# Last delta round computes five chunks of the output projection, heads in three slots by GpSimd's queue, semaphores cleared inside the phases

## The chip, the cores and the metric

The kernel runs on one core of a Trainium2 chip. The metric is the device time of one execution in microseconds. The engines are named PE (TensorE), DVE (VectorE), ACT (ScalarE), POOL (GpSimd) and SP (SyncE, which only issues DMAs here). Each runs its own queue of instructions in order, and waits on semaphores for the others.

## The reference

All in float32, on x of shape 4 x 512 x 512. Each of the four steps adds a layer-normalised result to x:

```python
x = x + ln(ssm(ln(x)))          # diagonal state space layer
x = x + ln(moe(ln(x)))          # 8 experts, top 2, and a shared one
x = x + ln(delta(ln(x)))        # below
x = x + ln(ffn(ln(x)))          # below
# delta: 16 heads of 128, 4 batches of 512 tokens
#   q,k,v = silu(conv(x @ W));  S = a*S - b*(S k - v) k^T;  o = S q
#   o = (layernorm(o) * ln_w + ln_b) * sigmoid(x @ Wg);  return o @ Wo      # Wo: 2048 x 512
# ffn: logits = x[batch].reshape(-1) @ switch_w.T + switch_b   (8 experts, over a whole batch of 512 tokens)
#   top 2 experts of the batch; per head of 32 columns: gelu(xh @ w1.T + b1) @ w2.T + b2, weighted, summed
#   return (x + o) @ w3.T + b3
```

## The kernel before

The tokens lie in 16 chunks of 128 tokens (NT = 16, TPB = 4 chunks a batch). The program is a sequence of phases: SSM, shared expert, routed experts, MoE output, delta, output. Each is a block in which every engine has a program of its own, and ends with a barrier of all engines. Names begin with a_, b_, x_, o_, c_ and d_ in that order. Between phases `retire_sems` opens one more block, in which GpSimd clears the semaphores of the phase that ended (L79), and all engines meet again (L75). That is done at four places.

The delta phase (`phase_delta`) works in 16 rounds, each of HG = 4 heads over one batch of 4 chunks, and stores the gated and transposed heads (c_oT) to the DRAM tensor ot_d. In its last round PE has no further projections to do; in their slots it computes the output projection (`out_part`) of chunks 0 to AHEAD - 1. One chunk is 16 heads x one matmul 128x512, four per weight tile (c_xs, c_w_k, c_w_q, c_w_v), here called a group. Its inputs are loaded into the tiles c_kT, c_qT, c_vT, its result sits in a PSUM bank c_ps_pj and is kept by ACT in c_conv. The end of the last round is, for each of the four chunks of batch 3: DVE's statistics, ACT's `norm_apply` (L1887), POOL's `gate_out` (L1563, three operations: times ln_w, plus ln_b, times the gate), PE's `turn_out` (transposes, L1670), ACT's `store` (L1876, L1879).

The output phase (`phase_out`) takes the chunks in order. PE: `outputs(n)` (the remaining projections, L2324, into yo[n % 2]), `turn(n)` (transposes of the normalised x, L2334), `route_logits(b)` after a batch, `chosen_experts(b)`, and the last layer. DVE per chunk: statistics of y (d_y_st), the residual add into d_x (L2521), statistics of x, and eight products with the switch weights (d_product, L2509), which make the routing logits; per batch the choice of experts (`choose`, d_w_sel, d_w_diag). ACT: the roots and the two activations per chunk (d_yn, d_xn), the copies of transposes and the gelus. `outputs(n)` waits until chunk n - 2 is normalised (y_normed), since that frees its bank. The experts of batch 0 stand inside chunk EARLY = 14. SP loads heads for chunk n + 2 once chunk n - 1 or so is projected (L2247), in one queue with the stores of x (L2258), and loads the switch weights, 2 MB for each of four parts.

Of the kernel before, what the change touches and what calls it, by code (L numbers as in the profile page):

```python
# [51 lines left out]
AHEAD = 3  # L52


class Program:


    def __init__(self, nc, io):
        self.nc, self.io = nc, io
        self.lasting = ExitStack()  # L60
        self.waits_passed = self.lasting.enter_context(nc.semaphore("waits_passed"))
        self.phase_sems = []
# [10 lines left out]
    def retire_sems(self):  # L73

        with self.nc.Block() as block:  # L75
            @block.gpsimd
            def _(e):
                for s in self.phase_sems:
                    e.sem_clear(s)  # L79
        for s in self.phase_sems:  # L80
            self.nc.release_semaphore(s)
        self.phase_sems = []
# [541 lines left out]
def phase_moe_shared(pr, con, XT, w_gu, gu_loaded, rt):  # L624
# [3 lines left out]
    with ExitStack() as st:  # L628
# [66 lines left out]
        def _(e):  # L695
# [23 lines left out]
            e.dma_start(rt.token[:, :], io["slot_token"].rearrange("(p t) o -> p (t o)", p=P)).then_inc(token_loaded, 16)  # L719

# [284 lines left out]
class DeltaInput:  # L1005
# [13 lines left out]

    def heads_out(self, n):  # L1020
        tile = self.heads["kqv"[n]] if n < AHEAD else self.heads["kq"[n % 2]]
        return tile[:, :, :].rearrange("p h (c m) -> p (h c) m", m=P)


def phase_moe_out(pr, con, XT, rt, tab, first):
# [6 lines left out]
    with ExitStack() as st:  # L1032
# [62 lines left out]
        def _(e):  # L1095
            for b in range(NB):
                if b >= 2:
                    e.wait_ge(y_done, TPB * (b - 1))
                for c in range(TPB):
                    for k in range(2):  # L1100
                        n = b * TPB + c
                        e.indirect_dma_start(picked[b % 2][k][:, c, :], None, io["y_slots"].rearrange("t p d -> (t p) d"),
                                             bass.IndirectOffsetOnAxis(rt.slot[:, k, n:n + 1], 0)).then_inc(picked_loaded[b % 2][c], 16)

# [222 lines left out]
def phase_delta(pr, con, XT, tab, given):  # L1327
# [15 lines left out]
    with ExitStack() as st:  # L1343
# [88 lines left out]
        ahead_bank = [pj[0], pj[1], pj[0]]  # L1432
# [13 lines left out]
        def _(e):  # L1446
# [63 lines left out]
            e.wait_ge(ahead_ready, 2)  # L1510
            load_ahead(3)
            e.wait_ge(ot_stored, rounds_before(NR - NB + 2))
            load_ahead(4)
            for n in (3, 4):
# [3 lines left out]
        def _(e):  # L1518
# [61 lines left out]
            def tail(r, buf):  # L1580
                a_round(r, buf, last=True)
                for c in range(TPB):
                    gate_out(r, buf, c)
# [23 lines left out]
            rounds(e, lambda r, buf, half: a_round(r, buf), tail)  # L1607

        @block.tensor
        def _(e):  # L1610
# [39 lines left out]
            def out_part(n, of):  # L1650
                for h in of:
                    if h == 0:
                        e.wait_ge(ahead_loaded[n], 16)
                        if n == 0:
                            e.wait_ge(conv_step, TAP_STEPS * (CONVS * (NR - 1) + CONVS + 1))
                        else:
                            e.wait_ge(g_copied, TPB * (NR - 1) + HG - 2 + n)
# [15 lines left out]
            def a_round(r, buf, half, last=False):  # L1673
# [3 lines left out]
                def next_unit(u, halves_=(0, 1)):  # L1677
# [4 lines left out]
                    for half_ in halves_:  # L1682
                        h = v * HG + half_ * HG // 2
                        if h < AHEAD * NH:
                            out_part(h // NH, range(h % NH, h % NH + HG // 2))
# [160 lines left out]
            def tail(r, buf):  # L1846
                a_round(r, buf, None, last=True)
                for c in range(TPB):
                    turn_out(r, c)

# [3 lines left out]
        def _(e):  # L1854
# [35 lines left out]
            def keep(n):  # L1890
                e.wait_ge(ahead_ready, n + 1)
                e.activation(conv[:, n, :], ahead_bank[n][:, :], ACT.Copy).then_inc(ahead_kept, 1)
# [851 lines left out]
```

## Time and profile before

| what | value |
|---|---|
| median of 3 runs | 3209.87 us (3209.33 to 3214.2) |
| the profiled execution's own time | 3214.72 us |
| span in its trace | 3213.0 us |
| mean granted TensorE clock | 0.950 |
| barriers that end the SSM, routed experts, MoE output and delta phases | 455.7, 1093.4, 1223.5, 2870.5 us |
| output phase | 2876.6 us to 3213.0 us |

Start times are counted from the first instruction of the span. A new phase begins a few microseconds after each of the four barriers.

### The profile page before, as it was taken

The numbers are of one execution on the slowest core, as the hardware profiler recorded it, in microseconds if no ns is written. First come the engines' busy times: TensorE is split into PE (matmuls) and PEld (weight loads), VectorE is DVE, ScalarE is ACT, GpSimd is POOL, SyncE is SP. The second block draws the span as 40 slices with busy tenths as digits, with TensorE's granted clock in tenths as the row PEclk, the third lists the DMA queues.
The fourth block names the chain that finished last, engine by engine and source line by source line (L and its number), as shares of the span: only waits on it lengthen the run. The fifth ranks groups of instructions, "written<-read, shape, count | busy, mean of one in ns | idle before, by whom it ended". The sixth has DMA issues, their size and how long they took to land. (4 is left out here: it accounts for less than half of the span.)

```text
span 3213.0 us, 42340 instructions
## 1 busy us (share of the span) xinstructions
PE 2944.2 (92%) x13274; PEld 1661.0 (52%) x13275; DVE 1882.8 (59%) x4723; ACT 1204.9 (38%) x2189; POOL 625.9 (19%) x759
## 2 busy tenths in 40 slices
PE   7899979997999588999999999999999999968998
PEld 3344444444666344666556665566555665533443
DVE  5767741000111276777787777867788777626766
ACT  3545500001222145444554445534554354422232
POOL 1111203101111312122222223222231222320000
PEclk9999968998999889999999999999999999979999
DMA  3000142003222451001100011000110001225312
GB/s 118 26 14 27 40 176 96 20 13 124 65 65 65 159 215 68 1 28 54 44 24 15 28 53 44 24 15 28 50 45 27 15 28 50 80 79 195 106 36 92
DMA packets 77123, 197.09 MB, mean 61 GB/s; under 512 B 11376, under 2 KB 12032, under 8 KB 70272
## 3 DMA queue, kind: packets, MB, share of 16 engines
q1 hardware_dynamic: 59744, 158.84, 13.8%
q0 software_dynamic: 6816, 18.92, 1.8%
q10 hardware_dynamic: 10368, 16.83, 1.4%
q8 instruction: 111, 1.82, 0.2%
q14 instruction: 84, 0.69, 0.1%
HBM read 137.90 MB, written 56.66 MB: 61 GB/s over the span
## 5 line engine op out<-in xcount | busy, mean ns | idle before, releaser
L2027 DVE SCALAR_TENSOR_TENSOR c_conv<-c_ps_pj,c_conv_t,c_conv 128x511 f32<-128x511 f32 (+2 forms) x495 | 367.9, 746 | 86.3 <-ACT c_conv L1866 74.7
L1647 PE MATMUL c_ps_pj<-c_w_g,c_xs 128*128 128x512 f32 x512 | 227.6, 592 | 0.0
L1630 PE MATMUL c_ps_pj<-c_xs,c_w_v 128*128 128x512 f32 x480 | 225.8, 593 | 0.0
L1630 PE MATMUL c_ps_pj<-c_xs,c_w_k 128*128 128x512 f32 x480 | 216.0, 593 | 2.9 <-DMA c_xs<-xt_d 2.9
L1630 PE MATMUL c_ps_pj<-c_xs,c_w_q 128*128 128x512 f32 x360 | 192.4, 668 | 2.2 <-DVE c_conv L2027 2.0
L1866 ACT ACTIVATE c_conv<-c_ps_pj,c_conv_t 128x512 f32<-128x512 f32 x165 | 127.8, 775 | 90.5 <-PE c_ps_pj L1630 83.9
L997 DVE TENSOR_TENSOR x_act<-x_hs,x_ps_u 128x352 f32<-128x352 f32 x40 | 20.9, 521 | 226.9 <-ACT x_hs L982 226.9
L1647 PEld LDWEIGHTS c_ps_pj<-c_w_g,c_xs 128*128 128x128 f32 x512 | 94.8, 190 | 107.1 <-issue 107.1
L2042 DVE TENSOR_TENSOR c_block_t<-c_block_L,c_block_X 128x126 f32<-128x126 f32 (+22 forms) x496 | 137.4, 277 | 18.5 <-DVE c_block_X L2046 1.8
L2046 DVE TENSOR_TENSOR c_block_X<-c_block_X,c_block_t 128x126 f32<-128x126 f32 (+22 forms) x496 | 137.6, 277 | 17.0
L850 DVE TENSOR_TENSOR b_act<-b_hs,b_ps_u 128x512 f32<-128x512 f32 (+1 forms) x24 | 16.5, 686 | 205.9 <-PE b_ps_u L742 205.9
L1630 PEld LDWEIGHTS c_ps_pj<-c_xs,c_w_k 128*128 128x128 f32 x480 | 86.5, 190 | 89.2 <-issue 86.1
L1920 ACT ACTIVATE c_err<-c_negL 32x128 f32<-32x128 f32 x256 | 78.6, 307 | 135.2 <-DVE c_negL L2115 130.5
L1696 PE MATMUL c_ps_kk<-c_kT 128*128 128x128 f32 x512 | 102.8, 283 | 26.3 <-DVE XT L2117 16.1
L261 PE MATMUL a_ps_pj<-XT,a_w_in 128*128 128x512 f32 x256 | 121.3, 619 | 3.5 <-DVE a_conv L486 2.7
L241 POOL TENSOR_SCALAR a_skip<-a_xc,a_col_d 128x512 f32<-128x512 f32 x32 | 62.6, 1956 | 316.3 <-ACT a_xc L355 174.3
L948 PE MATMUL x_ps_g<-b_w_gu,x_xT 128*128 x320 | 122.4, 464 | 1.4 <-ACT x_xT L973 0.8
L949 PE MATMUL x_ps_u<-b_w_gu,x_xT 128*128 x320 | 122.0, 463 | 0.0
L1563 POOL TENSOR_TENSOR XT<-XT,c_ln_w 128x512 f32<-128x512 f32 x64 | 81.2, 1269 | 195.3 <-DVE c_block_L L2048 157.5
L267 PE MATMUL a_ps_gt<-XT,a_w_gate 128*128 128x512 f32 x256 | 115.3, 593 | 2.5 <-ACT a_th L347 2.5
L1696 PEld LDWEIGHTS c_ps_kk<-c_kT 128*128 128x128 f32 x512 | 82.4, 195 | 64.1 <-DVE XT L2117 35.4
L284 PE MATMUL a_ps_yo<-a_w_out,a_th 128*128 128x512 f32 x256 | 115.5, 603 | 0.0
(433 smaller groups left out, 6094.3 us busy)
## 6 DMA issues: line engine op xcount, KB each, us to landing
c_xs<-xt_d SPq DMA_DIRECT2D x16, 1024.0 KB, 4.9
ot_d<-c_oT ACTq DMA_DIRECT2D x64, 256.0 KB, 2.0
b_w_gu<-in_w_gu SPq DMA_DIRECT2D x8, 1408.0 KB, 23.6
y_slots<-x_y SPq DMA_DIRECT2D x40, 256.0 KB, 2.0
a_x<-in_x SPq DMA_DIRECT2D x8, 1024.0 KB, 6.5
c_qT<-ot_d SPq DMA_DIRECT2D x8, 1024.0 KB, 5.6
d_x<-x SPq DMA_DIRECT2D x32, 256.0 KB, 2.9
d_switch<-in_switch_w SPq DMA_DIRECT2D x4, 2048.0 KB, 14.7
```

What stands on the lines that cost most here:

```text
L261: mm = e.matmul(pj[c % 2][:, :], w_in[:, k, c * P:(c + 1) * P], XT[:, b, k, :], start=(k == 0), stop=(k == KD - 1))
L267: mm = e.matmul(gt[:, :], w_gate[:, k, c * P:(c + 1) * P], XT[:, b, k, :], start=(k == 0), stop=(k == KD - 1))
L284: mm = e.matmul(yo[t % 2][:, :], th[:, b % 2, c, t * P:(t + 1) * P], w_out[:, c, :], start=(c == 0), stop=(c == CT - 1))
L948: e.matmul(g_ps[par][:, 0:FE], xT[par][:, k, :], w_gu[:, expert, k, 0:FE], start=(k == 0), stop=(k == KD - 1))
L949: mm = e.matmul(u_ps[par][:, 0:FE], xT[par][:, k, :], w_gu[:, expert, k, FE:2 * FE], start=(k == 0), stop=(k == KD - 1))
L1630: mm = e.matmul(bank_of[xb][u][:, :], w["kqv"[u // HG]][:, k, (u % HG) * DH:(u % HG + 1) * DH], xs[xb][:, k, :], start=(k == 0), stop=(k = ...
L1647: mm = e.matmul(pj[(xb + i) % 2][:, :], xs[xb][:, k, i * P:(i + 1) * P], w["g"][:, k, :], start=(k == 0), stop=(k == KD - 1))
L1696: e.matmul(kk[:, h, :], chunk(kT, h, c), chunk(kT, h, c), start=True, stop=True)
L1866: e.activation(conv[:, u % 4, :], bank_of[buf][u][:, :], ACT.Identity, bias=conv_t[buf][:, m, h, TAPS:TAPS + 1], scale=conv_t[buf][:, m, h ...
L2027: e.scalar_tensor_tensor(oc, bank_of[buf][u][:, 0:SEQ - s], conv_t[buf][:, m, h, TAPS - 1 - s:TAPS - s], oc, ALU.mult, ALU.add).then_inc(c ...
L2042: e.tensor_tensor(t, block_L[:, i + 1:BB, i].unsqueeze(2).to_broadcast([P, n, k]), block_X[:, i, 0:k].unsqueeze(1).to_broadcast([P, n, k]) ...
L2046: e.tensor_tensor(below, below, t, ALU.add).then_inc(sub_step, 1)
```

## The change

- Clearing: `retire_sems` has no block of its own; the semaphores of a phase are cleared by GpSimd at the end of its program in the phase after (`clear_retired`), in the shared expert's, the MoE output's and the delta phase. The delta phase's own are not cleared.
- AHEAD is 5. The last delta round computes chunks 0 to 4; part of chunk 3 and all of chunk 4 stand between and behind the transposes of the last round. Chunk 4 is kept in c_w_g.
- The last round's gating is DVE's.
- Heads for chunks 7 to 15 are loaded by GpSimd's queue into three tiles.
- In the output phase chunks 5 to 10 have a PSUM bank each (six banks), later ones alternate; transposes have fixed places among the groups; the experts of batch 0 stand before chunk 13 and wait until chunk 10 is normalised; ACT's and DVE's part of them stands before chunk 11; ACT does the y activation of chunk n before it copies the transposes of n - 1.
- w3 is loaded after the store of chunk 5.

```diff
-AHEAD = 3
+AHEAD = 5
     def retire_sems(self):
-        with self.nc.Block() as block:
-            @block.gpsimd
-            def _(e):
-                for s in self.phase_sems:
-                    e.sem_clear(s)
-        for s in self.phase_sems:
+        for s in self.cleared_sems:
             self.nc.release_semaphore(s)
-        self.phase_sems = []
+        self.cleared_sems, self.retired_sems, self.phase_sems = [], self.phase_sems, []
+    def clear_retired(self, e):
+        for s in self.retired_sems:
+            e.sem_clear(s)
+        self.cleared_sems, self.retired_sems = self.retired_sems, []
...
+    @staticmethod
+    def slot_out(n):
+        return "kqv"[n % 3] if n < 11 else "kq"[(n + 1) % 2]
+    def kept_out(self, n):
+        return self.conv[:, n, :] if n < 4 else self.w["g"][:, n - 4, :]
...
-        ahead_bank = [pj[0], pj[1], pj[0]]
+        ahead_bank = [pj[n % 2] for n in range(AHEAD)]
...
             def tail(r, buf):
                 a_round(r, buf, None, last=True)
-                for c in range(TPB):
+                out_part(3, range(HG, NH))
+                for c in range(2):
                     turn_out(r, c)
+                out_part(4, range(NH // 2))
+                for c in range(2, TPB):
+                    turn_out(r, c)
+                out_part(4, range(NH // 2, NH))
...
                 for c in range(TPB):
                     norm_apply(r, c)
+                keep(3)
                 for c in range(TPB):
                     store(r * TPB + c, ot_round[r, c])
+                keep(4)
...
-    EARLY = NT - 2
+    EARLY = AHEAD + 6
...
+        ring = [yo[0], yo[1], h_ps[0], h_ps[1], o_ps[0], o_ps[1]]
+        bank = {n: ring[n - AHEAD] if n < AHEAD + 6 else yo[(n - AHEAD) % 2] for n in range(AHEAD, NT)}
...
+            for n in range(AHEAD + 2, NT):
+                last_user = max(m for m in range(n) if given.slot_out(m) == given.slot_out(n))
+                if last_user >= AHEAD:
+                    e.wait_ge(yo_ready, last_user + 1)
+                e.dma_start(given.heads_out(n).rearrange("p (g h) m -> p g h m", h=HG),
+                            io["ot_d"].rearrange("g b c p h m -> b c p g h m")[n // TPB, n % TPB]).then_inc(heads_loaded[given.slot_out(n)], 16)
...
                 if of[0] == 0:
-                    e.wait_ge(heads_loaded[n % 2], 16 * (n // 2 + 1))
                     if n >= AHEAD + 2:
+                        e.wait_ge(heads_loaded[given.slot_out(n)], 16 * loads_of(n))
+                    if n >= AHEAD + 8:
                         e.wait_ge(y_normed, n - 1)
+                    elif n >= AHEAD + 6:
+                        e.wait_ge(y_normed, n - 5)
...
+                if b == 0:
+                    e.wait_ge(y_normed, AHEAD + 6)
...
+            turned_before = {HG + 3 * v: v for v in range(NT - 4)}
+            turned_before.update({10 * HG: NT - 4, 10 * HG + 2: NT - 3})
+            logits_after = {(9, 1): 0, (12, NG - 1): 1, (14, NG - 1): 2}
...
+                scale_y(n)
                 if n > 0:
                     take_turned(n - 1)
-                scale_y(n)
```

On PE, at the end of the delta phase, before the change (c_ps_kk is the last matmul of the round, c_ps_d the transposes of `turn_out`, L1343 the end of the phase):

```order
1004 L1823 MATMUL c_ps_z<-XT,c_R 128x128 x4
1005 L1840 MATMUL c_ps_kk<-c_err,XT 128x128 x4
1006 L1670 MATMUL c_ps_d<-ident,XT 128x128 x16
1007 L1343 UNCONDITIONAL_BRANCH
1008 L2316 UNCONDITIONAL_BRANCH
```

and with the change (c_ps_pj is the output projection, of chunk 3 from c_kT and of chunk 4 from c_qT):

```order
1004 L1832 MATMUL c_ps_z<-XT,c_R 128x128 x4
1005 L1670 MATMUL c_ps_pj<-c_xs,c_kT 128x512 x2
1006 L1849 MATMUL c_ps_kk<-c_err,XT 128x128 x4
1007 L1670 MATMUL c_ps_pj<-c_xs,c_kT 128x512 x2
1008 L1670 MATMUL c_ps_pj<-c_w_k,c_kT 128x512 x4
1009 L1670 MATMUL c_ps_pj<-c_w_q,c_kT 128x512 x4
1010 L1670 MATMUL c_ps_pj<-c_w_v,c_kT 128x512 x4
1011 L1680 MATMUL c_ps_d<-ident,XT 128x128 x8
1012 L1670 MATMUL c_ps_pj<-c_xs,c_qT 128x512 x4
1013 L1670 MATMUL c_ps_pj<-c_w_k,c_qT 128x512 x4
1014 L1680 MATMUL c_ps_d<-ident,XT 128x128 x8
1015 L1670 MATMUL c_ps_pj<-c_w_q,c_qT 128x512 x4
```

The transposes, one run of 16 before, now stand in two runs of 8 with 8 matmuls of chunk 4 between them and 8 behind (the last row and one more like it).

On PE, where the experts of batch 0 stand in the output phase, before (d_ps_h and d_ps_o are the experts' two layers, c_kT holds chunk 14's heads):

```order
1068 L2341 MATMUL d_ps_logits<-d_part,ones 128x32
1069 L2324 MATMUL d_ps_yo<-c_xs,c_kT 128x512 x4
1070 L2324 MATMUL d_ps_yo<-c_w_k,c_kT 128x512 x4
1071 L2324 MATMUL d_ps_yo<-c_w_q,c_kT 128x512 x4
1072 L2348 MATMUL d_ps_h<-XT,d_w_diag 128x512 x4
1073 L2359 MATMUL d_ps_o<-c_conv,d_w_diag 128x512 x2
```

and with the change (c_qT holds chunk 12's heads, c_kT chunk 13's):

```order
1060 L2361 MATMUL d_ps_tp<-ident,d_xn 128x128 x4
1061 L2351 MATMUL d_ps_yo<-c_w_v,c_qT 128x512 x4
1062 L2368 MATMUL d_ps_logits<-d_part,ones 128x32
1063 L2375 MATMUL d_ps_h<-XT,d_w_diag 128x512 x4
1064 L2386 MATMUL d_ps_o<-c_conv,d_w_diag 128x512 x2
```

The experts moved from chunk 14's last group to the place between chunks 12 and 13, right behind the second batch's logits.

On POOL, at the end of the delta phase and the start of the output phase, before:

```order
242 L1563 TENSOR_TENSOR XT<-XT,c_gate 128x512
243 L1343 UNCONDITIONAL_BRANCH
244 L76 UNCONDITIONAL_BRANCH
245 L79 ISA x78
246 L75 UNCONDITIONAL_BRANCH
247 L2307 UNCONDITIONAL_BRANCH
248 L2310 MEMSET d_r_prefer 128x1 x8
```

and with the change (the ISA rows are the clears):

```order
223 L1572 TENSOR_TENSOR XT<-XT,c_gate 128x512
224 L82 ISA x38
225 L1352 UNCONDITIONAL_BRANCH
226 L2325 UNCONDITIONAL_BRANCH
227 L2328 MEMSET d_r_prefer 128x1 x8
228 L2329 MEMSET d_same_head 128x128
229 L2332 MEMSET d_same_head 32x32 x4
230 L2337 DMA c_qT<-ot_d 128x4x512
231 L2337 DMA c_vT<-ot_d 128x4x512
232 L2337 DMA c_kT<-ot_d 128x4x512
```

The 78 clears are gone, 38 stand before the end of the phase, and nine loads of heads follow the memsets, of which three are shown.

## Rows read from the trace of the kernel before

**Rows 1.** The page: busy time, share of the span and instructions of each engine.

```profile
PE 2944.2 (92%) x13274; PEld 1661.0 (52%) x13275; DVE 1882.8 (59%) x4723; ACT 1204.9 (38%) x2189; POOL 625.9 (19%) x759
```

**Rows 2.** Barriers and clears by line: duration ns, then first and last start in us.

```profile
L137 PEldq EVENT_SEMAPHORE  x1: 51/51/51, 455.7 to 455.7; - x1
L858 PEldq EVENT_SEMAPHORE  x1: 51/51/51, 1093.4 to 1093.4; - x1
L1032 PEldq EVENT_SEMAPHORE  x1: 51/51/51, 1223.5 to 1223.5; - x1
L1343 PEldq EVENT_SEMAPHORE  x1: 51/51/51, 2870.5 to 2870.5; - x1
L79 POOLq EVENT_SEMAPHORE_RANGE_CLEAR  x188: 44/44/48, 455.8 to 2876.0; - x188
L75 PEldq EVENT_SEMAPHORE  x4: 51/51/51, 458.7 to 2876.6; - x4
```

**Rows 3.** The timeline behind two barriers: start us, us, engine, line, operation.

```profile
1096.10 0.40 SPq L1071 DMA_DIRECT2D o_shared<-y_shared  x1
...
1226.57 0.34 SPq L1447 DMA_DIRECT2D c_ln_w<-in_ln_w  x1
```

**Rows 4.** The timeline of the delta phase's end; in brackets the idle time before.

```profile
2840.38 1.16 PE L1840 MATMUL c_ps_kk<-c_err,XT 128*128 128x128 f32 x8 [0.69 <-ACT c_err L1979]
...
2847.88 6.26 ACT L1887 ACTIVATE XT<-XT,c_o_nb,c_o_rs 128x128 f32<-128x128 f32 x16 [7.06 <-DVE c_o_nb L2094]
...
2853.93 1.12 PE L1670 MATMUL c_ps_d<-ident,XT 128*128 128x128 f32 x4 [12.39 <-POOL XT L1563]
...
2864.94 1.26 POOL L1563 TENSOR_TENSOR XT<-XT,c_gate 128x512 f32<-128x512 f32 x1 [0.18 <-POOL XT L1563]
...
2866.26 1.11 PE L1670 MATMUL c_ps_d<-ident,XT 128*128 128x128 f32 x4 [2.99 <-POOL XT L1563]
2867.41 0.60 ACT L1876 ACTIVATE c_oT<-c_ps_d 128x512 f32<-128x512 f32 x1 [3.51 <-PE c_ps_d L1670]
```

**Rows 5.** The timeline of PE in the output phase's first 46 us.

```profile
2876.74 6.47 PE L2324 MATMUL d_ps_yo<-c_xs,c_qT 128*128 128x512 f32 x8 [9.37 <-SPq L2277]
...
2912.40 0.66 PE L2334 MATMUL d_ps_tp<-ident,d_xn 128*128 128x128 f32 x4 [4.27 <-ACT d_xn L2432]
2922.22 5.93 PE L2324 MATMUL d_ps_yo<-c_xs,c_qT 128*128 128x512 f32 x8 [9.16 <-DMA c_qT<-ot_d]
```

**Rows 6.** The timeline of ACT (first row) and DVE in the output phase.

```profile
2876.63 1.28 ACT L2463 ACT_TABLE_LOAD   x1 [8.62 <-PEq L75]
...
2890.70 0.69 DVE L2509 SCALAR_TENSOR_TENSOR d_product<-d_xn,d_switch 128x512 f32<-128x512 f32 x1 [6.64 <-DMA d_switch<-in_switch_w]
...
2976.76 0.42 DVE L2558 TENSOR_TENSOR d_chosen<-d_w,d_r_one 128x256 f32<-128x256 f32 x1
...
2982.61 0.69 DVE L2490 BATCH_NORM_STATS2 d_y_st<-d_ps_yo 128x6 f32<-128x512 f32 x1
...
2987.36 0.69 DVE L2521 TENSOR_TENSOR d_x<-d_x,d_yn 128x512 f32<-128x512 f32 x1 [0.98 <-ACT d_yn L2432]
...
2991.70 0.15 DVE L2496 SCALAR_TENSOR_TENSOR d_x_nb<-d_x_mv,d_x_rs 128x1 f32<-128x1 f32 x1
```

**Rows 7.** The chain that ended last, in order of time: start us, us, what.

```profile
2982.15 13.74 PE d_ps_yo L2324 x32
...
3077.68 3.43 PE d_ps_yo L2324 x8
...
3095.33 0.71 DVE d_y_st L2490
```

**Rows 8.** Windows: us, busy time of each engine, granted clock, DMA share, GB/s.

```profile
2854.00:2870.00 16.00, 4.39 (x16) 2.79 (x16) 0.00 (x0) 2.53 (x5) 11.13 (x9) 0.50 0.17 66
2884.00:2908.00 24.00, 24.00 (x63) 10.77 (x61) 12.09 (x35) 5.05 (x12) 0.00 (x0) 1.00 1.04 369
```

**Rows 9.** DMA issues: out<-in, engine, count, KB each, median us to landing.

```profile
c_qT<-ot_d SPq DMA_DIRECT2D x8, 1024.0 KB, 5.6
...
x_x<-xn,x_one_token POOLq DMA_INDIRECT x40, 3.4
...
c_w_g<-in_w SPq DMA_DIRECT2D x1, 1024.0 KB, 15.4
```

More of the change, by code:

```diff
@@ L1509, in _ @@
             load_ahead(2)
-            e.wait_ge(ahead_ready, 2)
-            load_ahead(3)
             e.wait_ge(ot_stored, rounds_before(NR - NB + 2))
-            load_ahead(4)
-            for n in (3, 4):
+            for n in range(3, AHEAD + 2):
+                e.wait_ge(ahead_ready, n - 2)
+                load_ahead(n)
+            for n in (AHEAD, AHEAD + 1):
                 e.wait_ge(ahead_loaded[n], 16)
@@ L1891, in keep @@
                 e.wait_ge(ahead_ready, n + 1)
-                e.activation(conv[:, n, :], ahead_bank[n][:, :], ACT.Copy).then_inc(ahead_kept, 1)
+                e.activation(given.kept_out(n), ahead_bank[n][:, :], ACT.Copy).then_inc(ahead_kept, 1)
             ot_round = io["ot_d"].rearrange("g b c p h m -> (g b) c p h m")
@@ L2175, in tail @@
                     norm_part(r, c)
+                e.wait_ge(ln_loaded, 32)
+                for c in range(TPB):
+                    n = r * TPB + c
+                    e.wait_ge(o_normed, HG * n + HG)
+                    e.wait_ge(g_done, n + 1)
+                    for i, (b, op) in enumerate(((over_heads(ln_w), ALU.mult), (over_heads(ln_b), ALU.add), (gates[buf][:, c], ALU.mult))):
+                        if i > 0:
+                            e.wait_ge(o_gated, 3 * n + i)
+                        e.tensor_tensor(o[:, c], o[:, c], b, op).then_inc(o_gated, 1)
             rounds(e, a_round, tail)
@@ L2221, in phase_out @@
         o_ps = [ps(f"o{i}", [P, SEQ]) for i in range(2)]
-        z_ps = [yo[0], yo[1], o_ps[0], o_ps[1]]
-        heads_loaded = [sem(f"heads_loaded{i}") for i in range(2)]
+        z_ps = [yo[1], yo[0], o_ps[0], o_ps[1]]
+        ring = [yo[0], yo[1], h_ps[0], h_ps[1], o_ps[0], o_ps[1]]
+        bank = {n: ring[n - AHEAD] if n < AHEAD + 6 else yo[(n - AHEAD) % 2] for n in range(AHEAD, NT)}
+        heads_loaded = {m: pr.swdge_sem(f"d_heads_{m}_loaded") for m in "kqv"}
+        loads_of = lambda n: sum(given.slot_out(m) == given.slot_out(n) for m in range(AHEAD + 2, n + 1))
         x_loaded = [sem(f"x_loaded{c}") for c in range(TPB)]
@@ L2239, in phase_out @@
         block = st.enter_context(nc.Block())
-        source = lambda n: kept[:, n, :] if n < AHEAD else yo[n % 2][:, :]
+        source = lambda n: given.kept_out(n) if n < AHEAD else bank[n][:, :]
         row = lambda name, n: io[name][n // TPB, n % TPB * P:(n % TPB + 1) * P, :]
```

66 lines of the change are left out of this document (24 added, 42 removed).

## The prediction

> **What bounds the kernel now.** I read the page first: TensorE (PE) is busy 92% of the span, VectorE (DVE) 59% [rows 1]. So only two things can shorten the kernel: stretches in which PE does nothing, and PE work at less than full clock. I then went to the four places the diff touches and read, at each, which wait ends last.
>
> The first kind is the end of a phase. By the rows of the barriers, all engines have met at 455.7, 1093.4, 1223.5 and 2870.5 us, then GpSimd clears 188 semaphores, and the next phase begins at 458.7, 1096.1, about 1226.5 and 2876.6 [rows 2, 3]. Nothing else runs there. The four gaps are 2.94, 2.68, 2.96 and 6.08 us, 14.66 in all; the second and third ends are those of the next phase's first DMA issue less some 0.06.
>
> The second is the end of the delta phase. PE's last real matmul group starts at 2840.38; DVE's statistics end at 2847.9, ScalarE (ACT) normalises, and POOL gates each chunk in three operations of 1.27 us, 4.1 us a chunk. Each transpose waits for that, the last store follows 2867.4, and the barrier is at 2870.5 [rows 4]. PE is busy 4.4 of 16 us, its clock at 0.50, the lower of its two levels [rows 8].
>
> The third is the output phase up to chunk 15's last matmul, when its statistics start (3095.33 [rows 7]): 218.7 us from 2876.6. A chunk costs PE 13.74 us, and the experts of the first batch half from 3063.76 to 3077.68, 13.9 us [rows 7]. PE's work is 13 x 13.74 + 15 turns x 0.44 + 13.9 + 0.6 for logits = 199.7. The rest: a wait of 4.27 us for ACT and one of 9.16 us for chunk 5's heads [rows 5], together 13.4, and groups of 8 matmuls at low clock, 6.47 and 5.93 us where 3.43 (13.74 / 4) is normal, 3.0 + 2.5 = 5.5. That adds up to 218.6. DVE meanwhile needs 9.27 us per chunk (2982.61 to 2991.85), 5.9 us to choose a batch's weights and some 3.8 for its routing [rows 6], so it stays under PE's 14.2 a chunk and waits for it.
>
> **The change, term by term.**
>
> *Clears.* 110 of the clears move behind GpSimd's last instruction of three phases; the delta phase's 78 vanish. GpSimd has long been idle at the end of the first two, and in the last its work shrinks, since the 12 gating operations leave it. Covered by PE's remaining work, they cost nothing; uncovered, 38 would cost about 3 us each time. I take -14.7.
>
> *Delta tail.* Added to PE: two chunks of output projection, 2 x 13.74 = 27.5, of which 4 matmuls lie in the last round's slots. After the last group at 2840.4 stand 12 (10.3 us at full clock, to about 2854 since the first few are slow). Gating on DVE: 12 x 0.73 (the 128x512 operation of 0.69 with its issue [rows 6]) = 2.2 us a chunk, chunk 0 done near 2852.7, the last at 2859.3, instead of 2853.9 and 2866.2. So the transposes are ready before PE wants them. PE then runs: two transposes, half a chunk 6.87, two transposes, 6.87, to 2872.3, ACT's copy 0.6, barrier 2873.4: +2.9. The stores of the transposed heads land earlier than before, which costs nothing here.
>
> *Output phase.* PE's work falls by 2 x 13.74 to 172.2. Whether that is gained depends on DVE, which keeps all 16 chunks: 16 x 9.27 + 3 x 9.7 for routing and choosing + 3.0 for adding the first expert result = 180, more than PE's 172. So the bound moves from PE to DVE, and PE begins to wait for it. I walked both queues through the printed orders, t counted from the phase's first instruction. DVE cannot start its products before 14.1 (the switch weights land, 2890.70 [rows 6]); it ends chunk 2's statistics start at 23.0 and goes on in steps of 9.3 to chunk 5 at 50.8. It then needs the first logits, which PE has queued behind 18 groups (a group is the matmuls of 4 heads, 3.43 us, and five turns of 0.44 lie between them), so not before 64.4: 4 to 5 us of DVE lost. Chunk 6 starts at 65.1, 7 at 77.3, 8 at 92.4 (choosing lies ahead), 9 at 101.6; the second logits hold DVE from 110.9 to 117.3; 10 starts at 118.1. Its y is normalised 4.7 later (2982.61 to 2987.36 [rows 6]), at 122.8. PE stands at 116.9 before the first batch's experts, which now wait for just that: **5.6 us**. ACT can serve their gelus only after chunk 10's second activation and a table load of 1.28 [rows 6], near 130: **5.6** again. Chunk 13's matmuls wait for chunk 11 to be normalised (142.9 + 4.7 = 147.6): **5.5**. Chunk 14's wait for chunk 12 (162.1 + 4.7 = 166.8): **5.1**. With 2.5 at the ninth turn the waits are 24.3, so PE finishes chunk 15 at 172.2 + 24.3 = 196.5. Waits of this length are followed by slow groups: the 9.16 us wait cost 2.5, and I take 2 after each of the four, 8 in all (from 0 to 12). 204.5 against 218.7: **-14.1**. What follows chunk 15 (117.7 us to the end) is unchanged, since the last choice hangs on chunk 15 alone.
>
> *Heads by GpSimd's queue.* These 1 MB loads took 5.6 us from SyncE's queue; GpSimd's queue moved only gathers in this trace, 3.4 us from a 0.97 us issue [rows 9]. No row has a 1 MB load on it. Lower bound 3.4, upper bound by the slowest 1 MB load here, 15.4 us beside the switch weights. The loads are issued one or two chunks ahead, 13.7 us at least, 27 for chunks 7 and 8, and GpSimd has nothing else to do; the walk loses nothing up to 15 us. I take 0. The Trainium skill (SBUF — State Buffer, Who interferes with whom) says that the descriptors of a DMA from GpSimd's queue are written by GpSimd itself, and that it is locked out of the shared port pair, and the DMA starved, while DVE runs an operation of its two-port modes. That speaks against this edit, and no row here shows it for such a load; if it held through most of DVE's work the load would miss its lead, which is rival E. Also, chunk 7's load now starts at once beside the first switch weights; at 369 GB/s [rows 8] 1 MB is 2.8 us, which could delay DVE's start by 0 to 2.8.
>
> Sum: -14.7 + 2.9 - 14.1 = -25.9. The profiled execution took 3214.72 us (span 3213.0), 4.9 above the median of 3209.87; from the median it gives 3184.0 (about 3189 if profiled as before).
>
> **The rivals.**
>
> *A, the forecast, DVE and ACT pace the phase: 0.60.*
>
> *B, PE stays the bound.* Waits and slow groups vanish altogether: 218.7 - 172.2 = -46.5 and the sum is -58, 3152. For it: PE never waited long for DVE before, once saturated. Against it: the count 180 against 172, and the two logits queued late. 0.05.
>
> *C, the waits come but the clock stays full:* -22 in the phase, 3176. For it: the 4.27 us wait was not followed by a measurable slow group before the next wait. 0.13.
>
> *D, the first three gaps give nothing* (2.94 + 2.68 + 2.96 = 8.6): the phase end moves by the same amount, because the clears are now on the path to the barrier or slow GpSimd's last work. For it: after the clears GpSimd still has to reach the barrier. Against it: in the rows the next phase's first DMA issue comes right after the gap [rows 3], so everything behind it moves up. 3192. 0.14.
>
> *E, the other side: heads come late.* If a 1 MB load by GpSimd's queue takes longer than its lead, every chunk from 9 on pays the excess. Shifting the landings in the walk: 20 us costs 4, 25 costs 14, 30 costs 26, and the balance with before is near 30 us; at 35 the kernel is 24 slower, 3234. For it: an unmeasured queue and DVE working beside it all the time. Against: 3.4 us for gathers while DVE worked too. The page's rule is this case's mechanism; by the figures beside it (about 620 ns alone, 3100 ns beside a DVE operation) a load would come some 2.5 us late, which is an estimate and inside the lead. 0.04 for over 30, 0.04 for 20 to 30 (3188 to 3209).
>
> **How the numbers follow.** The prediction is A's, 3184. A's own range: slow groups 0 to 12 (-8, +4), DVE's start +2.8, tail +-2: 3176 to 3191. The range of 3171 to 3196 adds C and D and leaves out B, E and the far ends of A. The measurement tells 0.2%, 6.4 us. Slower by more is E beyond 30 us: 0.04. Within 0.2% are parts of E and a sum of D with full slow groups: 0.05. Faster: 0.91.
>
> **What would show it.** Barriers followed within 0.1 us by the next phase's first instruction, four times. The delta phase lasting 2 to 4 us longer than the 1644.0 from 1226.5 to 2870.5, with no GpSimd wait before the transposes, PE busy to the end and its clock at 1.0 there. In the output phase: no wait for chunk 5's heads; about five waits of PE, the four named ones of 5 to 6 us in the last third, for DVE and ACT, not for DMA; DVE waiting for logits twice; heads landing in under 14 us. I would be wrong if PE waits for heads at chunks 9 to 15 (E), if the waits are absent (B), or if the time before the experts is much longer than 11 us, in which case the walk, and not a price, failed.

## The result and the profile after

The changed kernel takes **3183.34 us** (median of 4 runs, 3180.8 to 3191.16) against 3209.6 us before (median of 4): a ratio of 0.9925, 95% interval 0.9909 to 0.9941, so 24 us faster by the ratio and 26 by the medians. The forecast was 3184.0. The profiled execution is the first and slowest of the four: 3191.16 us, span 3189.4, mean clock 0.954; the spans differ by 23.6 us.

The barrier that ends the delta phase and the first rows of the output phase, in the changed kernel's trace (in the manner of [rows 2, 5]):

```profile
L1352 PEldq EVENT_SEMAPHORE  x1: 51/51/51, 2866.8 to 2866.8; - x1
```

```profile
2866.87 1.28 ACT L2485 ACT_TABLE_LOAD   x1 [0.27 <-PEq L1352]
2867.06 1.96 PE L2351 MATMUL d_ps_yo<-c_xs,c_vT 128*128 128x512 f32 x4 [1.09 <-PEq L1352]
```

The next phase begins 0.1 us behind the barrier, where 6.1 us lay. The first three phase ends show the same: their barriers come at 455.2, 1089.3 and 1216.8 us, and the next phases' first DMA issues at 455.26, 1089.37 and 1216.87 (before: 458.76, 1096.10 and 1226.57 [rows 3]). GpSimd's 110 clears run from 581.8 to 2807.1 us, the last of them 60 us ahead of the delta phase's barrier: they are covered.

PE at the end of the delta phase, timeline, in answer to [rows 4]. A matmul leaves two records, so a group of four matmuls is an x8 in these rows:

```profile
2835.00 1.05 PE L1849 MATMUL c_ps_kk<-c_err,XT 128*128 128x128 f32 x8
2835.89 1.88 PE L1670 MATMUL c_ps_pj<-c_xs,c_kT 128*128 128x512 f32 x4
...
2844.47 3.60 PE L1670 MATMUL c_ps_pj<-c_w_v,c_kT 128*128 128x512 f32 x8
2847.91 0.60 PE L1680 MATMUL c_ps_d<-ident,XT 128*128 128x128 f32 x4
2849.76 0.63 PE L1680 MATMUL c_ps_d<-ident,XT 128*128 128x128 f32 x4 [1.25 <-DVE XT L2200]
2850.22 3.60 PE L1670 MATMUL c_ps_pj<-c_xs,c_qT 128*128 128x512 f32 x8
...
2858.47 0.63 PE L1680 MATMUL c_ps_d<-ident,XT 128*128 128x128 f32 x4 [0.78 <-ACT c_oT L1890]
...
2862.37 3.60 PE L1670 MATMUL c_ps_pj<-c_w_v,c_qT 128*128 128x512 f32 x8
```

The 12.39 us in which PE had nothing to do are filled, and its clock is 1.00 where it was 0.50 [rows 8]. Both waits, 1.25 and 0.78, are for ACT: `turn_out` writes all chunks into one bank, c_ps_d, and waits until ACT has copied the chunk before out of it. The row of the 1.25 names DVE, but VectorE had finished that chunk at 2848.32, while ACT's copy ended at 2849.61, 0.15 us before PE went on; the second copy ended at 2858.33:

```profile
2847.63 0.69 DVE L2200 TENSOR_TENSOR XT<-XT,c_gate 128x512 f32<-128x512 f32 x1
```

```profile
2849.03 0.58 ACT L1890 ACTIVATE c_oT<-c_ps_d 128x512 f32<-128x512 f32 x1
...
2857.73 0.60 ACT L1890 ACTIVATE c_oT<-c_ps_d 128x512 f32<-128x512 f32 x1 [2.81 <-PE c_ps_d L1680]
```

All waits of PE from there to chunk 15, by the view of waits (us in total, times, longest):

```profile
PE d_ps_yo L2351 <- ACT d_yn L2454: 10.5, 2, 5.5
PE d_ps_h L2375 <- ACT d_yn L2454: 5.6, 1, 5.6
PE d_ps_h L2375 <- ACT c_conv L2478: 3.7, 1, 3.7
PE d_ps_tp L2361 <- ACT d_xn L2454: 2.5, 1, 2.5
```

None is for heads. Where they stand, and the groups behind them, in the timeline:

```profile
2969.62 0.66 PE L2361 MATMUL d_ps_tp<-ident,d_xn 128*128 128x128 f32 x4 [2.46 <-ACT d_xn L2454]
2970.11 5.30 PE L2351 MATMUL d_ps_yo<-c_xs,c_qT 128*128 128x512 f32 x8
...
2991.93 3.75 PE L2375 MATMUL d_ps_h<-XT,d_w_diag 128*128 128x512 f32 x4 [5.64 <-ACT d_yn L2454]
2999.34 3.78 PE L2375 MATMUL d_ps_h<-XT,d_w_diag 128*128 128x512 f32 x4 [3.66 <-ACT c_conv L2478]
...
3019.79 6.33 PE L2351 MATMUL d_ps_yo<-c_xs,c_kT 128*128 128x512 f32 x8 [5.53 <-ACT d_yn L2454]
...
3041.83 5.37 PE L2351 MATMUL d_ps_yo<-c_xs,c_qT 128*128 128x512 f32 x8 [4.98 <-ACT d_yn L2454]
```

A row of 8 records is 3.60 long elsewhere, one of 4 is 1.88. The waits sum to 22.3 us, and the slow groups (with a 2.75 for 1.88 behind the second 3.78) to 10.8. The releaser named is ACT, but ACT itself waits for VectorE. The chain that ended last shows it for chunk 10, whose normalised y the experts wait for:

```profile
2990.14 0.70 DVE d_product L2531 x2
2991.01 0.79 ACT d_yn L2454
2991.89 0.70 DVE d_x L2543
...
2996.48 0.81 ACT d_xn L2454
2997.31 1.28 ACT L2488
2998.61 0.70 ACT c_conv L2478
2999.34 3.78 PE d_ps_h L2375 x4
```

And what VectorE waited for in the output phase up to chunk 15, beside 16.1 us in sixteen short waits for ACT's d_yn and the phase's start:

```profile
...
DVE c_vT L2611 <- PE d_ps_o L2386: 12.7, 4, 6.4
...
DVE d_logits L2558 <- PE d_ps_logits L2368: 11.2, 2, 8.3
DVE d_product L2531 <- DMA d_switch<-in_switch_w: 9.2, 2, 9.0
```

The row left out is 11.4 us for ACT's root of x (d_x_rs). The longest of these, 6.9 us at 3031, is PE's doing too: that root stands in ACT's queue behind a copy of transposes, for which ACT waited 10.38 us. No run below is aimed at it.

A single profile hides something that is needed to read such sums. From the first DMA issue of the delta phase to the start of the round's last 128x128 group lie 1613.8 us before (2840.38 less 1226.57, [rows 3, 4]) and 1618.1 after. Only 1.7 us of the difference are PE work that the change put there (two matmuls). In two of the experiments below the programs up to this point are the same to the instruction:

```profile
1214.86 0.35 SPq L1456 DMA_DIRECT2D c_ln_w<-in_ln_w  x1
...
2820.53 1.05 PE L1849 MATMUL c_ps_kk<-c_err,XT 128*128 128x128 f32 x8
```

```profile
1214.18 0.35 SPq L1456 DMA_DIRECT2D c_ln_w<-in_ln_w  x1
...
2835.62 1.05 PE L1849 MATMUL c_ps_kk<-c_err,XT 128*128 128x128 f32 x8
```

That is 1605.7 us in logits_early and 1621.4 in half_products. The windows over these two stretches (us, then busy time of PE, PEld, DVE, ACT and POOL, granted clock, DMA share, GB/s) show where the difference lies:

```profile
1214.86:2820.53 1605.67, 1541.54 (x9389) 957.89 (x9390) 1200.72 (x3067) 748.90 (x1415) 420.27 (x475) 0.98 0.10 36
```

```profile
1214.18:2835.62 1621.44, 1559.94 (x9388) 967.45 (x9389) 1201.18 (x3067) 748.79 (x1415) 419.82 (x475) 0.97 0.10 36
```

PE is busy 18.4 us longer with the same matmuls, VectorE, ACT and GpSimd within 0.5, and the granted clock is lower. So the long rounds scatter by 16 us from execution to execution, by TensorE's clock, while three short stretches repeat more closely: **the tail** (start of the last of those 128x128 matmuls to the output phase's first), **the stretch** (from there to where PE goes on behind chunk 15's last matmul), and **the end** (from there on). In all that follows the mechanisms are read from these and the totals from the medians. The stretch is from one execution of each kernel. Where its program is the same it still differs by up to 2.9 us: 218.4 and 216.6 (before, clears_only), 205.5, 206.6 and 203.7 (the change, clears_undone, gate_pool). Differences below 3 us between two stretches are therefore not read as effects.

| kernel | median us | ratio to before | tail | stretch | end |
|---|---|---|---|---|---|
| before | 3209.6 | 1 | 35.5 | 218.4 | 117.9 |
| the change | 3183.3 | 0.9925 | 31.3 | 205.5 | 116.9 |
| clears_only | 3193.6 | 0.9947 | 29.4 | 216.6 | 117.0 |
| clears_undone | 3196.1 | 0.9958 | 37.2 | 206.6 | 117.4 |
| logits_early | 3171.6 | 0.9887 | 31.3 | 194.9 | 116.8 |
| half_products | 3174.3 | 0.9881 | 31.3 | 195.6 | 111.9 |
| gate_pool | 3189.3 | 0.9940 | 36.9 | 203.7 | 116.9 |
| heads_sp5 | 3194.8 | 0.9966 | 31.3 | 219.3 | 116.8 |
| heads_sp3 | 3223.8 | 1.0056 | 31.3 | 244.4 | 116.7 |
| ahead4 | 3170.8 | 0.9898 | 25.0 | 199.4 | 115.3 |
| half_logits | 3161.8 | 0.9849 | 31.3 | 184.7 | 111.9 |
| mix_inside | 3166.8 | 0.9873 | 31.3 | 187.9 | 116.9 |
| combined | 3169.5 | 0.9885 | 25.0 | 196.5 | 117.0 |
| heads_sp7 | 3182.4 | 0.9923 | 31.3 | 203.3 | 116.8 |

### The profile page after: what moved, and what is told of

Its sections match the earlier page's. It is cut to its first block and busy times, and to the rows that moved or that the text cites. A ratio compares the mean times of both kernels' runs of the same rounds, so it can differ in the third digit from the quotient of the medians.

```text
span 3189.4 us, 42203 instructions
## 1 busy us (share of the span) xinstructions
PE 2948.7 (92%) x13274; PEld 1663.8 (52%) x13275; DVE 1892.3 (59%) x4735; ACT 1204.9 (38%) x2191; POOL 615.3 (19%) x756
## 5 line engine op out<-in xcount | busy, mean ns | idle before, releaser
L852 DVE TENSOR_TENSOR b_act<-b_hs,b_ps_u 128x512 f32<-128x512 f32 (+1 forms) x24 | 16.5, 686 | 205.9 <-PE b_ps_u L744 205.9
L1705 PE MATMUL c_ps_kk<-c_kT 128*128 128x128 f32 x512 | 104.3, 287 | 23.6 <-DVE XT L2133 15.1
L268 PE MATMUL a_ps_gt<-XT,a_w_gate 128*128 128x512 f32 x256 | 115.3, 593 | 2.7 <-ACT a_th L348 2.7
L1638 PEld LDWEIGHTS c_ps_pj<-c_xs,c_w_v 128*128 128x128 f32 x480 | 82.0, 191 | 57.4 <-issue 57.4
```

Source lines behind the costliest of these rows:

```text
L1638: mm = e.matmul(bank_of[xb][u][:, :], w["kqv"[u // HG]][:, k, (u % HG) * DH:(u % HG + 1) * DH], xs[xb][:, k, :], start=(k == 0), stop=(k = ...
L1705: e.matmul(kk[:, h, :], chunk(kT, h, c), chunk(kT, h, c), start=True, stop=True)
```

## The experiments

The theory: the clears were pure loss, the tail is covered work, and in the output phase VectorE (with ACT in its chain) sets the time. The rivals were that the clears' gaps give nothing (D), that PE or ACT paces by itself, and that GpSimd's queue costs something (E).

**clears_only.** The kernel before, with the new `retire_sems`, and the last line at the end of GpSimd's program in three phases (shared expert, MoE output, delta):

```diff
-        with self.nc.Block() as block:
-            @block.gpsimd
-            def _(e):
-                for s in self.phase_sems:
-                    e.sem_clear(s)
-        for s in self.phase_sems:
+        for s in self.cleared_sems:
...
+            pr.clear_retired(e)
```

> The kernel before, with the 188 clears dealt with as in the change and nothing else. Theory (the gap is only the clears and the second barrier): each of the four gaps (2.94, 2.68, 2.96, 6.08 us) closes, a phase's first instruction follows the barrier by under 0.1 us, and the time falls by 14.7 us, a ratio of 0.9954. Rival D (the first three give nothing): the gaps close but the phases get as much longer, and the time falls by 6.1 us, 0.9981.

0.9947 (0.9930 to 0.9964), 15.2 us by the medians. The tail falls by 6.1 us, all of the fourth gap. Rival D's 0.9981 lies outside the interval.

**clears_undone.** The changed kernel with the old `retire_sems`:

```diff
-        for s in self.cleared_sems:
+        with self.nc.Block() as block:
+            @block.gpsimd
+            def _(e):
+                for s in self.phase_sems:
+                    e.sem_clear(s)
+        for s in self.phase_sems:
...
-            pr.clear_retired(e)
...
```

> The changed kernel with the clears in blocks of their own again (the same 188 clears, 78 of them after the delta phase). Theory: it is 14.7 us slower than the changed kernel, near 3198, ratio to before 0.9964; the rest of the change alone is then worth 11 to 12 us. Rival D: only 6.1 slower than the changed kernel, near 3189.

3196.1, 12.8 slower than the change, the tail 5.9 longer. With clears_only this brackets the forecast's 14.7 from both sides: by the medians the clears are worth 13 to 15 us (by the ratios 11 to 17), and the rest of the change 10 to 13.

**logits_early.** Two instructions of PE move:

```diff
-            logits_after = {(9, 1): 0, (12, NG - 1): 1, (14, NG - 1): 2}
+            logits_after = {(8, 3): 0, (12, 0): 1, (14, NG - 1): 2}
```

> The changed kernel with two logits matmuls of PE (one instruction each) moved ahead: the first batch's from behind chunk 9's second group to behind chunk 8's last, the second batch's from behind chunk 12's last group to behind its first. Theory (VectorE paces the output phase, and its two waits for logits, 8.3 and 2.9 us, are passed on to PE): the waits of VectorE for logits go to under 1 us in sum, PE reaches the end of chunk 15 some 8 to 14 us earlier, and the time is about 3183 - 12 = 3171, ratio to before 0.988. Rival (PE or ACT paces it, or the waits of PE have causes of their own): no change, 3183.

3171.6, ratio 0.9887 (0.9870 to 0.9903). PE's work in the stretch is the same to the instruction, yet the stretch is 10.6 us shorter. The line of VectorE's waits for logits, 11.2 us in the change, is gone from the trace:

```profile
DVE d_x L2543 <- ACT d_yn L2454: 15.1, 15, 1.3
DVE d_y_st L2512 <- PEq L2420: 14.6, 1, 14.6
DVE c_vT L2611 <- PE d_ps_o L2386: 12.6, 4, 6.2
DVE d_x_nb L2518 <- ACT d_x_rs L2451: 11.4, 4, 6.8
DVE d_product L2531 <- DMA d_switch<-in_switch_w: 10.2, 2, 10.0
```

What counted was not PE's speed but its order: other work stood in front of what VectorE needed. VectorE's lost time came back at the end as PE's lost time, nearly one for one.

**half_products.**

```diff
-                    e.scalar_tensor_tensor(product[:, :], xn[n % 2][:, :], 1.0, switch[:, v, c * DM:(c + 1) * DM],
+                    e.scalar_tensor_tensor(product[:, :DM // 2], xn[n % 2][:, :DM // 2], 1.0, switch[:, v, c * DM:c * DM + DM // 2],
...
```

> The changed kernel with each of VectorE's 128 products with the switch weights made over 256 of the 512 columns (the logits lose half of their terms, so other experts can be chosen; the amount of their work is the same). A product goes from 0.69 to some 0.42 us. Theory (VectorE paces): chunk costs VectorE 9.27 - 8 x 0.27 = 7.1 us, PE's waits fall from 22.3 to about half, the phase up to chunk 15 is 10 to 12 us shorter, and what follows chunk 15 about 3 (its own products); 3169. PE does not get to no waits at all, as the logits still come late. Rival (PE or ACT paces): only the 3 us behind chunk 15, 3180.

The kernel leaves out half of the products' terms. The median is 3174.3 (ratio 0.9881) where 3169 was expected. The stretch is 9.9 shorter, the end 5.0 (5 instead of the 3 expected). This agrees with the theory, but less work should have given more: the 112 products in the stretch are busy for 47.1 us instead of 77.0, so 30 us of VectorE's work are gone. Its waits say where they went:

```profile
DVE d_logits L2558 <- PE d_ps_logits L2368: 18.4, 2, 12.5
DVE d_x_nb L2518 <- ACT d_x_rs L2451: 18.2, 6, 6.8
```

A faster engine that waits for an instruction at a fixed place in another's queue waits longer for it.

**half_logits.** Both edits.

> Both edits of logits_early and half_products together (each product over 256 of 512 columns, so the logits lose half of their terms). In half_products VectorE used what it gained to wait longer for logits (18.4 us instead of 11.2). Theory (VectorE's own work and its waits for logits are one chain that paces PE): with the logits early the halved products are worth their full size, the stretch from the output phase's start to chunk 15's last matmul goes from 194.9 us in logits_early to about 184 (PE's own work there is 172.2), and the time is near 3155 to 3158. Rival (after logits_early something else paces, ACT or PE with the experts): the stretch stays at 193 to 195 and only the 5 us behind chunk 15 are gained, 3166.

The stretch is 184.7, against 184 forecast, and the median 3161.8, above the 3155 to 3158. PE's waits in the stretch fall to 8.4 us, all for ACT's d_yn. Halving the products is worth 10.1 with the logits early (194.9 to 184.7) and 9.9 with them late (205.5 to 195.6); moving the logits is worth 10.6 with whole products and 10.9 with halved ones. The two gains add, which is what two parts of one chain do; that they agree to 0.3 us is closer than single profiles can tell. Of the 30 us of products still only 10 arrive: VectorE's waits for ACT's root of x are 25.1 us here, against 11.4 in logits_early.

**mix_inside.** logits_early, and

```diff
             def chunk(n):
...
                 if n > 0:
                     switch_part(n - 1, range(NE // 2))
+                if n == EARLY:
+                    mix(0)
                 shift(n, y_mv, y_rstd, y_rs, y_offset, y_nb)
...
             for n in range(NT):
-                if n == EARLY:
-                    mix(0)
                 chunk(n)
```

> logits_early, and VectorE's four adds of the first expert result moved from ahead of chunk 11's statistics to behind its statistics and the first four products. In the changed kernel VectorE waits 12.7 us for PE's and ACT's expert chain at these adds while work that hangs on nothing stands behind them. Theory: 3.8 us of that work (0.9 of statistics, 2.9 of products) fill the wait, the stretch up to chunk 15 is 3 to 4 us shorter than in logits_early, 191, and the time 3168. Rival (ACT's table loads and gelus pace this place, so chunk 11 is normalised no earlier): the stretch stays at 195.

187.9, 7.0 shorter than logits_early where 3 to 4 were expected, and 3166.8 (ratio 0.9873, 0.9853 to 0.9892). VectorE's wait for the experts' results is 8.1 us instead of 12.6, so chunk 11 is normalised earlier, and PE's wait ahead of chunk 13 shrinks. That row in logits_early and then in mix_inside:

```profile
2994.77 6.24 PE L2351 MATMUL d_ps_yo<-c_xs,c_kT 128*128 128x512 f32 x8 [5.54 <-ACT d_yn L2454]
```

```profile
2997.57 3.67 PE L2351 MATMUL d_ps_yo<-c_xs,c_kT 128*128 128x512 f32 x8 [1.87 <-ACT d_yn L2454]
```

The wait falls by 3.7 us, as forecast, and a wait of 1.87 is short enough that the group behind it is not slow, another 2.6. The group behind the next wait is 1.2 slower (6.62 for 5.37), and the waits of 0.79 and 4.27 in logits_early are 0 and 4.09, their slow groups 0.8 shorter in sum. So of the 3.3 us beyond the forecast wait, some 2 are TensorE's clock and 1 the small waits.

**gate_pool.** The last round's gating back on GpSimd:

```diff
                 a_round(r, buf, last=True)
+                for c in range(TPB):
+                    gate_out(r, buf, c)
...
-                            e.wait_ge(o_gated, 3 * n + i)
-                        e.tensor_tensor(o[:, c], o[:, c], b, op).then_inc(o_gated, 1)
```

> The changed kernel with the last round's gating on GpSimd again (3 x 1.27 us a chunk instead of 3 x 0.73 on VectorE). Theory: GpSimd delivers chunks 0 to 3 at 13.5, 17.6, 21.7 and 25.8 us after the last 128x128 group of the round starts, VectorE at 13.8 at the latest for chunk 1 in the changed kernel. PE has 10.3 us of chunk 3's projection before the first and 6.9 us of chunk 4's before the third, so it waits about 0.5, 3.5, 0 and 1 us instead of 1.25 and 0.78, and the delta phase ends 2 to 3 us later. Time 3186. Rival (the gating's speed decides the tail as in the kernel before): 4 x 1.9 = 7 to 8 us later, 3191.

The tail is 5.6 longer, between the forecast 2 to 3 and the rival's 7 to 8, and the median is 3189.3 against 3186 and 3191. The waits for GpSimd came as forecast (0.39 and 3.44), but the second one cost more than itself:

```profile
2850.41 1.11 PE L1682 MATMUL c_ps_d<-ident,XT 128*128 128x128 f32 x4 [3.44 <-POOL XT L1572]
2851.31 5.96 PE L1672 MATMUL c_ps_pj<-c_xs,c_qT 128*128 128x512 f32 x8
```

5.96 for 3.60, and 1.11 for the 0.63 of the transposes: PE runs at its lower level after the wait (granted clock 0.58 from 2851 to 2857). With VectorE gating, the longest wait was 1.25 and no group was slow.

**heads_sp5 and heads_sp3.** The nine loads move from GpSimd's to SyncE's queue (heads_sp3 has n + 3 for n + 5):

```diff
             for n in range(NT):
+                if AHEAD + 2 <= n + 5 < NT:
+                    load_heads(n + 5)
                 store_x(n)
...
-            for n in range(AHEAD + 2, NT):
...
```

> The changed kernel with the loads of heads 7 to 15 issued by SyncE, the load of chunk n + 5 ahead of the store of chunk n, nine loads in all with the waits they have now. It tells what GpSimd's queue as such costs (its loads land after 6.0 to 9.0 us in the changed kernel, against 5.4 for SyncE's before). Theory (both land inside the lead of 13.7 us or more): no change, 3183, no wait of PE for heads. Rival (GpSimd's queue costs time by the work of making descriptors or by the switch weights that it slows, 17.7 us instead of 14.7): 3 to 6 us faster.

> As heads_sp5, but the load of chunk n + 3 ahead of the store of chunk n. SyncE's queue is in order and a store waits for VectorE's residual add of its chunk, so the loads now come at VectorE's pace and not at PE's. Theory: PE waits for heads at nearly every chunk from 8 on, about 30 us slower than the changed kernel, 3213; this is what a separate queue for the loads is worth with three chunks of VectorE's lag. Rival (the queue's order is irrelevant, only the landing counts): 3183.

heads_sp5 missed its forecast of no change: 3194.8, with a stretch 13.8 longer. One load did it, chunk 7's, whose issue stood behind others in SyncE's queue (first fence), and PE waited for it (second; chunk 7's bank is d_ps_h):

```profile
2875.44 5.32 SPq L2280 DMA_DIRECT2D x<-d_x  x2
2889.50 0.32 SPq L2276 DMA_DIRECT2D d_x<-x  x1
2889.86 0.43 SPq L2302 DMA_DIRECT2D c_qT<-ot_d  x1
```

```profile
2895.97 6.35 PE L2354 MATMUL d_ps_h<-c_xs,c_qT 128*128 128x512 f32 x8 [11.39 <-DMA c_qT<-ot_d]
```

SyncE stood 8.7 us at the load ahead (L2276), which waits until the store of x of chunk 0 has landed. That store landed 14.0 us after its issue, 0.7 behind the last of 8 MB of switch weights that were issued ahead of it; such stores take 2.0 us in the median in the changed kernel. That the weights held it up is argued from this order, not tested by itself. The kernel before has the same knot, which the forecast did not see: there the wait of SyncE for that store is 11.2 us, and the load behind it is the one that PE waits 9.16 us for [rows 5]. In heads_sp3 chunk 7 costs 16.1, the three loads after it 5.4 to 6.9 each, and the kernel is slower than before. It is 40 us above the change where 30 had been said.

**heads_sp7.** heads_sp5 with chunk 7's load at the head of SyncE's queue:

```diff
+            load_heads(AHEAD + 2)
             load_x(0)
...
```

> heads_sp5 with the load of chunk 7 put at the head of SyncE's queue. In heads_sp5 it was issued at 2889.9, 34 us into the phase, since SyncE's issues of switch weights and expert weights took the time before; PE then waited 11.4 us for it, and that was the only wait for heads. Theory (the place in SyncE's queue was the whole cost): no wait for heads, the stretch up to chunk 15 back at 205 to 206 us, the time at 3183. Rival (SyncE's queue is worse for the later loads too): a wait for heads appears at a later chunk, above 3188.

3182.4, the stretch 203.3, no wait for heads. Both differences to the change (1.0 and 2.2 us) are within the scatter, so GpSimd's queue is worth nothing as such. Its worth is that nothing stands in front of the loads.

**ahead4.**

```diff
-AHEAD = 5
+AHEAD = 4
...
-                out_part(4, range(NH // 2))
                 for c in range(2, TPB):
                     turn_out(r, c)
-                out_part(4, range(NH // 2, NH))
...
-                keep(4)
...
-            logits_after = {(9, 1): 0, (12, NG - 1): 1, (14, NG - 1): 2}
+            logits_after = {(7, 3): 0, (11, 0): 1, (14, NG - 1): 2}
```

> The changed kernel with AHEAD 4: chunk 4's projection (13.74 us of PE) goes back to the output phase, experts of the first batch stand before chunk 12, and the logits stand behind chunk 7's last and chunk 11's first group, so that VectorE doesn't wait for them (as in logits_early, 3171.6). Theory (VectorE paces the output phase, so PE's work there is cheap, and costs its full length in the delta phase's tail once the gating no longer covers it): the delta phase ends 6 to 7 us earlier, the output phase up to chunk 15 is 8 to 9 us longer than in logits_early, in all 3172 to 3175. Rival (PE's work moved ahead is worth its length in the output phase): 13.7 longer there and 6.6 shorter in the tail, 3179.

3170.8, level with logits_early within the runs' scatter. The tail is 6.3 shorter, the stretch 4.5 longer than logits_early's, though PE has 13.74 us more to do in it; 8 to 9 had been expected. Not all logits are early in it: VectorE waits 8.7 us for a later batch's, and 19.0 for the experts. Even so, the fifth chunk ahead buys nothing once the first two batches' logits are early.

**combined.** ahead4 with mix_inside's edit and the first load by GpSimd behind chunk 4's projection:

```diff
-                if last_user >= AHEAD:
-                    e.wait_ge(yo_ready, last_user + 1)
+                if n == AHEAD + 2 or last_user >= AHEAD:
+                    e.wait_ge(yo_ready, max(last_user, AHEAD) + 1)
```

> ahead4 with the adds inside chunk 11's (here chunk 10's) work as in mix_inside, and the first load by GpSimd's queue behind chunk 4's projection instead of beside the first switch weights. Theory: 4 us less than ahead4 from the adds and up to 3 from the first switch weights landing earlier (17.7 us as the median of four in the changed kernel, 14.7 before); 3165. Rival: the two edits hit waits that others cover, 3171.

3169.5. The stretch is 2.9 shorter than ahead4's and the end 1.7 longer, so of the 4 + 3 expected 1.2 is left, which is within the scatter. VectorE's wait for the switch weights fell from 10.1 to 7.4 and that for the experts from 19.0 to 16.2, but the one for later logits rose from 8.7 to 9.5, and PE's longest wait for ACT's d_xn from 2.1 to 4.0. That these waits, with one chunk more of PE's work in the phase, hide what the edits gave is argued, not shown.

Of the versions that leave nothing out, mix_inside has the lowest median: 42.5 us below the kernel before and 16.5 below the change. Its interval overlaps those of logits_early, ahead4 and combined; that it is ahead of logits_early rests on its stretch, 7.0 us shorter.

## Why the prediction was right, step by step

- **Clears, -14.7.** Measured -15.2 alone and -12.8 within the change. Right. The trace gives 14.7 for the gaps; rival D is out.
- **Delta tail, +2.9.** The tail fell by 4.2, of which 6.1 are the gap, so +1.9, and 1.7 for the two matmuls ahead of it less a wait of 0.69 that vanished: +2.9. The mechanism held (the gaps filled, the gating covered, the clock full); that the size came out to 0.1 us is luck, since errors cancel. The walk put 12 matmuls behind the last 128x128 group where 14 stand (1.7 too little), two more ahead of it at nothing (1.0, with the wait), and saw no wait for ACT's copies out of the one bank (2.0). Against that it allowed some 2.3 for a slow start that did not come, and its 2872.3 needs transposes of 1.1 us each, as in [rows 4], where its own 0.44, which the trace shows, gives 2869.5 (2.7 too much). The stated sign of it, a delta phase 2 to 4 us longer between its barriers, was not seen: it was 5.9 longer (1216.87 to 2866.8). Of that 3.3 (the 4.3 up to the last 128x128 group less the 1.0 of work there) lie in rounds that the change did not touch and which scatter by 16; the rest, 2.6, is inside the 2 to 4. That criterion was badly chosen.
- **Output phase, -14.1.** -12.9 measured. PE's work is 172.2 by the forecast's count; with the waits of 22.3 and the slow groups of 10.8 it makes 205.3 against 205.5 in the trace. Four of the five waits were forecast to 0.1 us (2.5, 5.6, 5.5, 5.1 against 2.46, 5.64, 5.53, 4.98). Their places were not: PE reached the experts at 119.2 us into the phase and not at 116.9, mostly by the slow group behind the 2.5 wait, which the walk left out, and chunk 10 was normalised at 124.7 and not at 122.8. VectorE's two waits for logits were 2.9 and 8.3 where the walk had 4 to 5 and 6.4. PE and VectorE came late together, so the waits between them kept their size. The one for ACT's gelus was 3.66 instead of 5.6: PE's first expert matmuls ran at its lower level, 3.75 us for the 1.88 of the walk, and so used up 1.9 us of the wait. The slow groups were mis-sized the other way, 10.8 for 8: each of the four waits of over 3 us cost 1.8 to 2.8, and the wait of 2.46 another 1.7. (The forecast's price, 2.5 for the wait of 9.16, should be 2.3: it took 3.43 from a row that is 3.60 long at the full clock.) What follows chunk 15 was taken as unchanged and is 1.0 shorter; clears_only, which has the old program there, has 117.0 too, so this is scatter.
- **VectorE paces.** logits_early, half_products and half_logits show it. A PE-only account cannot have the stretch shrink by 10 at constant PE work. It is a chain of engines and the place of one instruction, and not VectorE's speed alone: halving its largest work gave 10 of 30 us.
- **Heads by GpSimd's queue, 0.** Right, and rival E is out. 1 MB landed in these times (median us, last number):

```profile
c_qT<-ot_d POOLq DMA_DIRECT2D x4, 1024.0 KB, 7.1
...
c_kT<-ot_d POOLq DMA_DIRECT2D x4, 1024.0 KB, 6.0
c_vT<-ot_d POOLq DMA_DIRECT2D x1, 1024.0 KB, 9.0
```

One by one, the four loads that ran beside or soon behind the switch weights took 12.6, 9.0, 9.0 and 8.4 us, the five later ones 5.7 to 6.1, where SyncE's had a median of 5.6 [rows 9]. The longest, chunk 7's, is beyond the 6.0 to 9.0 that the expectation of heads_sp5 gives, but inside its lead of some 27 us. VectorE was busy 67% of the phase up to chunk 15. The Trainium skill (SBUF — State Buffer, Who interferes with whom) has such a load starved while VectorE runs an operation of its two-port modes; it names copy, cast and tensor_scalar, and says that tensor_tensor has no such mode. VectorE ran products, additions, statistics and reductions here, and the five later loads were late by at most 0.5 us, which agrees; whether the rule holds for the operations that it names, no run here shows. The cause of the old wait for heads, the knot at the store of chunk 0, was missing from the forecast.
- **VectorE's start.** First product 15.0 us into the phase against 14.1 assumed and 14.0 before (14.1 from the barrier): within the 0 to 2.8 given. heads_sp7, with the load of chunk 7 issued by SyncE ahead of the switch weights, has 12.9.
- **Rival C** (no slow groups) is out, the granted clock being 0.55 from 2992 to 3006 us. **B** is out, and nothing tried reached its 172 us; half_logits came nearest with 184.7.
- The median fell on the forecast within 1 us, more closely than the terms did, and that much is luck. Their errors (output phase +1.2, clears up to 2, the cancelling ones of the tail) are smaller than the scatter of the rounds.

## What to carry to other kernels

When two engines' totals are close (180 against 172 us here), walk both queues through the printed order and look for a tiny instruction of the faster one that the slower one waits for. Moving two such instructions was worth about as much (11.8 us) as all of the change but the clears (10 to 13). Then ask what each load stands behind in its queue, above all a wait for a store to land, before asking how fast the queue is. And compare profiles stretch by stretch, with the granted clock of each: one pair of spans may differ by as much as a change of this size is worth.

## What the runs showed of the hardware

A wait of 3.44 us with PE otherwise busy was followed by a slow group (5.96 for 3.60 us, gate_pool), and one of 2.46 too (5.30; granted clock 0.72 from 2970 to 2976); waits of 1.25 and 1.87 were not. The 9.16 us wait before cost 2.3 [rows 5] and the 11.39 of heads_sp5 2.75, while two waits of 4.98 cost 1.8 (the change) and 3.0 (mix_inside): in these traces the price does not follow the wait's length.

Identical code for 15 rounds took 1605.7 and 1621.4 us in two executions, 1%, with no engine's program changed. The granted clock was 0.98 and 0.97, and PE busy for 1541.5 and 1559.9 us.

Issuing from SyncE took 0.32 to 0.65 us for most transfers. While the switch weights were under way single issues took much longer: 3.98 and 3.74 us for one switch part and for c_w_g before the change, and 4.68 and 5.32 for two switch parts and two stores in heads_sp5. So a queue can be late by its own issues. GpSimd's took 0.75 to 0.87 in the changed kernel.
